# A gated recurrent scan of 512 steps: start-up with a plain float32 input product, a first step without matmuls, and the low parts of the recurrent weights made later

## The chip, the cores and the metric

The kernel runs on one core of a Trainium2 chip. The metric is the device time of one execution in microseconds (us); the time before is the median of three runs. The engines are TensorE (PE in the profile; its weight loads are PEld), VectorE (DVE), ScalarE (ACT), GpSimd (POOL) and SyncE (SP), which issues most of the DMAs. Matmul results land in PSUM, in eight banks of 512 float32 columns; everything else lives in SBUF, with 128 partitions.

## The reference

Two layers act on `x` of 4 x 512 x 256. The first is a gated recurrence over the 512 positions, followed by a feed-forward layer; the second is a mixture of dense experts and a routed layer with 64 experts. Only the recurrence matters here:

```
xz, xr, xh = seq @ W_z, seq @ W_r, seq @ W          # for all positions
vz, vr, vh = video @ C_z + b_z, video @ C_r + b_r, video @ C + b
def step(h, xs):
    z = sigmoid(xzt + h @ U_z + vz)
    r = sigmoid(xrt + h @ U_r + vr)
    hh = tanh(xht + r * h @ U + vh)
    h_new = (1 - z) * h + z * hh
h0 = zeros                                          # 4 x 256
```

`seq` is x (batch 4, 512 steps, width 256) and the state h has 4 x 256 values. Each step needs the state of the step before.

## The kernel before

**Layout.** Features lie on partitions, so the state is 128 partitions x 8 columns (two halves of the width, four of the batch). The steps are cut into spans of 40, the last one of 32. For each span the three input products (gates r, z and candidate, two halves of the output each, so `GROUPS` = 6 products of 160 columns) are made one span ahead and put, scaled and with their biases, into PSUM banks 0 to 5 (`pre`: one pair of banks for each gate, even and odd spans taking turns). The recurrent products are then added to them there.

**Precision.** Float32 inputs are split in two: W and x into a high part in the reduced format float32r (made by ACT, `W_part[0]`, `x_part[0]`) and the remainder (made by DVE, `W_part[1]`, `x_part[1]`, by `low_weights` and `low_inputs`). A product is then three matmuls (`MEET`): high x high, low x high, high x low. `input_product` yields 6 x 2 x 3 = 36 of them for a span. The recurrent weights U are scaled by a power of two and split into float16: `Us[:, g, 0]` by ACT (L419), `Us[:, g, 1]` by DVE (L609). A recurrent product (`recur`) is 12 matmuls of 4 columns: 8 for the high part of the state with both parts of U, 4 for its low part.

**Start-up** (nothing recurrent runs yet). TensorE: clears banks with a product of ones and zeros (`clear(0)`, L804), condition product (L838, 12 matmuls of 4 columns), biases (L843), then the input product of span 0 (L889 to L896) into banks 6 and 7. Two small products are worked in between: after 12 of the 36 matmuls the turning of the peaks of |U| (L892), after 24 the product with ones that spreads the scales to all partitions (L895). Then come `clear(1)`, a wait for all three low parts of U (`s_ulo`) and one for all six seeded products (`s_first`). DVE: low parts of inputs and weights (L544, L549), peaks of U (L557), bias sums (L561, L563), the chain that makes scales out of peaks (L567 to L582), their reading from PSUM (L586 to L589), `vb` (L593), then alternately a scaled copy of an input product into `pre` (`first_span`, L600) and a low part of U (L609), three pairs, then three more copies, then `low_inputs` of span 1. ACT: high parts of inputs and weights (L409, L415), high parts of U (L419).

**A step** (the loops from L489, L749 and L905). TensorE adds to the r gate's columns the step's own part (L908, L910) and then the state's product for z (L913, L915); ACT takes tanh for r (L493) and twice for z (L495, L496) and scales z (L498); DVE makes (1 + r) h, high and low (L755, L617), and the kept part (1 - z) h (L762, L764, L768); TensorE multiplies the reset state with U for the candidate (L929, L931), ACT takes its tanh (L500), DVE makes z times candidate, high and low (L772, L773, L617) and the new state in its several forms (L781 to L792). TensorE also adds the kept part's product for the next r (L945, L947), one matmul of the next span's input product in each step (`ahead`), and in later spans the feed-forward layer's matmuls of the span before. Semaphores `s_rp`, `s_zp`, `s_cp` tell ACT that r, z and candidate are ready in PSUM. Every engine works its queue in the order of the source; that order is written out by hand.

## Time and profile before

| | us |
|---|---|
| median of 3 runs | 2144.11 (2141.66 to 2145.39) |
| the profiled execution | 2145.97 |
| its span, first to last instruction | 2144.2 |
| TensorE busy in the span | 2104.4 (98%) |
| DVE busy | 1577.6 (74%) |
| ACT busy | 1014.0 (47%) |
| first recurrent tanh (ACT, L493) | starts at 22.09 |
| spacing of the first steps | 1.99 |

The span runs from the first to the last instruction of the profiled execution. "Busy" means that the engine has an instruction in flight; TensorE's instructions overlap one another, so the share says that work is recorded, not that the array is full. A start time in a row is counted from the start of the span. Where an instruction had to wait, a row has in brackets how long the engine was idle before it and who released it. The clock line of the page gives the granted TensorE clock in 40 equal slices, 9 standing for nine tenths or more of the full 2.4 GHz.

### The profile page before, as it was taken

To read this page: it belongs to the slowest core of one execution; us is meant where nothing else is said; L and a number is where in the kernel's file an instruction comes from. 1 tells how busy PE (TensorE), PEld (TensorE's weight loads), DVE (VectorE), ACT (ScalarE), POOL (GpSimd) and SP (SyncE) were. 2 spreads that over 40 slices of the span, in tenths; PEclk is the share of its full clock that TensorE was granted. 3 is DMA by queue.
4 is the path that set the end of the run, shared out by engine and by line. 5 is a ranking of instruction groups with operands and counts; after the bars stand their busy time and mean duration, and the time that the engine had idled before them with its cause. 6 is when DMAs were issued, how large, how long until landed. Compare 5 with 4: busy or idle time off the path is not lost. (4 is left out here: it accounts for less than half of the span.)

```text
span 2144.2 us, 83054 instructions
## 1 busy us (share of the span) xinstructions
PE 2104.4 (98%) x32793; PEld 1974.3 (92%) x32801; DVE 1577.6 (74%) x8997; ACT 1014.0 (47%) x3950; POOL 432.2 (20%) x593
## 2 busy tenths in 40 slices
PE   8999999999999999999999999999999999999997
PEld 7899999999999999999768888766999999999997
DVE  6887877877887887778745555592777777777775
ACT  3555555555555555555555777532222222222221
POOL 0000000000000000000000000444455555555553
PEclk9999999999999999999999999999999999999999
DMA  3001000000000000000003322313888888888882
GB/s 126 4 4 44 4 4 4 4 4 4 4 4 4 4 4 4 4 4 4 3 1 106 100 79 79 128 48 139 274 274 269 282 269 272 284 264 277 280 263 58
DMA packets 55559, 213.73 MB, mean 100 GB/s; under 512 B 11578, under 2 KB 40960, under 8 KB 46976
## 3 DMA queue, kind: packets, MB, share of 16 engines
q1 hardware_dynamic: 36276, 184.41, 23.5%
q0 software_dynamic: 17408, 23.61, 5.8%
q8 instruction: 257, 4.21, 0.8%
q14 instruction: 134, 1.10, 0.2%
q10 hardware_dynamic: 1484, 0.40, 0.1%
HBM read 192.82 MB, written 15.57 MB: 97 GB/s over the span
## 5 line engine op out<-in xcount | busy, mean ns | idle before, releaser
L1849 PE MATMUL bank<-xe,ring 128*128 128x160 f32 x3072 | 438.6, 299 | 0.7 <-DVE xe L1899 0.7
L1849 PEld LDWEIGHTS bank<-xe,ring 128*128 128x128 f32 x3072 | 422.9, 190 | 0.9 <-issue 0.9
L1892 DVE STREAM_TRANSPOSE turned<-ye 32x64 f32<-32x64 f32 x1240 | 291.4, 235 | 16.2
L854 PEld LDWEIGHTS bank<-keep_part,Us 128*128 128x128 f16 x6132 | 276.5, 111 | 1.8 <-DVE keep_part L768 0.4
L854 PE MATMUL bank<-keep_part,Us 128*128 128x4 f16 x6132 | 260.0, 170 | 0.5 <-DVE keep_part L768 0.3
L1877 ACT ACTIVATE gate_f<-bank 128x160 f32<-128x160 f32 x384 | 116.4, 303 | 285.8 <-PE bank L1849 278.3
L854 PE MATMUL bank<-raw,Us 128*128 128x4 f16 x6144 | 241.9, 167 | 2.0 <-issue 1.1
L1804 POOL DMA_INDIRECT out_rows<-res,to_row x128 | 192.3, 1503 | 234.2 <-DVE res L1911 201.6
L493 ACT ACTIVATE r_h<-bank 128x8 f32<-128x8 f32 x512 | 92.3, 180 | 292.0 <-PE bank L854 292.0
L523 POOL TENSOR_TENSOR hist<-ring,unscale 128x128 f32<-128x128 f32 x32 | 16.4, 513 | 1042.2 <-DVE ring L786 1042.2
L1858 PE MATMUL bank<-mid,ring 128*128 128x160 f32 x1536 | 220.9, 300 | 2.1 <-issue 2.1
L1858 PEld LDWEIGHTS bank<-mid,ring 128*128 128x128 f32 x1536 | 213.5, 191 | 2.3 <-issue 2.3
L823 PE MATMUL bank<-in_part,W_part 128*128 128x160 f32 (+1 forms) x468 | 215.3, 474 | 0.0
L1920 DVE TENSOR_TENSOR mid<-bank,gate_f 128x160 f32<-128x160 f32 x384 | 117.6, 318 | 130.8 <-ACT gate_f L1877 123.3
L854 PEld LDWEIGHTS bank<-raw,Us 128*128 128x128 f16 x6144 | 210.1, 105 | 2.5 <-DVE raw L792 1.3
L854 PE MATMUL bank<-rh_high,Us 128*128 128x4 f16 x4096 | 206.3, 172 | 2.9
L854 PE MATMUL bank<-step_high,Us 128*128 128x4 f16 x4096 | 189.5, 168 | 3.8 <-issue 0.8
L854 PEld LDWEIGHTS bank<-rh_high,Us 128*128 128x128 f16 x4096 | 165.1, 112 | 26.6 <-DVE rh_high L755 14.7
L498 ACT ACTIVATE z_cand<-tz,lift 128x8 f32<-128x8 f32 x512 | 155.5, 304 | 16.5
L854 PEld LDWEIGHTS bank<-step_high,Us 128*128 128x128 f16 x4096 | 148.6, 105 | 9.2 <-DVE step_high L772 2.6
L772 DVE TENSOR_TENSOR step_high<-z_cand 128x8 f16<-128x8 f32 x512 | 89.2, 174 | 80.2 <-ACT z_cand L500 70.7
L1097 PE MATMUL bank<-x_part,weights_part 128*128 128x512 f32 x576 | 136.7, 395 | 2.2 <-DVE x_part L1288 2.2
(275 smaller groups left out, 4042.2 us busy)
## 6 DMA issues: line engine op xcount, KB each, us to landing
ring<-in_ew SPq DMA_DIRECT2D x64, 2304.0 KB
raw<-in_L_cond_ew SPq DMA_DIRECT2D x16, 1024.0 KB, 6.6
ctx_rows<-rows SPq DMA_DIRECT2D x2, 1280.0 KB, 6.7
dense_w<-in_L_ffn_W SPq DMA_DIRECT2D x2, 1024.0 KB, 9.3
dense_w<-in_L_cond_sw SPq DMA_DIRECT2D x2, 1024.0 KB, 6.5
out_rows<-orow SPq DMA_DIRECT2D x4, 512.0 KB, 2.9
out_rows<-res,to_row POOLq DMA_INDIRECT x128
xT<-in_xT SPq DMA_DIRECT2D x2, 864.0 KB, 10.0
```

Of the source, the lines that this page charges most:

```text
L493: nc.scalar.activation(r, pre_of(0, q, jj), ACT.Tanh, scale=inv[0]).then_inc(s_r, 1)
L498: nc.scalar.activation(z, tz[:], ACT.Identity, scale=2.0 ** (STATE_EXP - 1), bias=lift[:, 0:1]).then_inc(s_z, 1)
L772: nc.vector.tensor_tensor(step_high[:, :, 2], z, cand, ALU.mult).then_inc(s_shi, 1)
L823: last = nc.tensor.matmul(product(span, n), W_part[w][:, g, k, m * P:(m + 1) * P], steps_of(x_part[x], span)[:, k], start=(k == 0 and i == ...
L854: last = nc.tensor.matmul(pre[g][q][:, jj, m, :], Us[:, g, p, k, m * P:(m + 1) * P], x[part][:, k * B:(k + 1) * B], start=False, stop=Fals ...
L1097: last = nc.tensor.matmul(up[f % len(up)][:], w[i][:, k, f * P:(f + 1) * P], x[j][:, k], start=(k == 0 and i == 0 and j == 0), stop=(k == ...
L1804: nc.gpsimd.indirect_dma_start(out=out[:, :], out_offset=bass.IndirectOffsetOnAxis(ap=to_idx[c][:, 0:1], axis=0), in_=res[e % 2][c][:], in ...
L1849: last = nc.tensor.matmul(bank[f % UPS][:, s_ * CAP:(s_ + 1) * CAP], w1[u][:, k, s_ * FFN + f * P:s_ * FFN + (f + 1) * P], xe[e % 2][:, k] ...
L1858: last = nc.tensor.matmul(bank[6 + e % 2][:, d * CAP:(d + 1) * CAP], w2[u][:, f, d * P:(d + 1) * P], mid[e % 2][:, f], start=(f == 0), sto ...
L1877: nc.scalar.activation(gate[:, f % 2], bank[f % UPS][:, CAP:2 * CAP], ACT.Silu).then_inc(s_silu, 1)
L1892: last = nc.vector.transpose(y[:, :, q, :], ye[e % 2][q * SQ:(q + 1) * SQ, :, j * SQ:(j + 1) * SQ])
L1920: nc.vector.tensor_tensor(mid[e % 2][:, f], bank[f % UPS][:, 0:CAP], gate[:, f % 2], ALU.mult).then_inc(s_mid, 1)
```

## The change

Three things are changed, all in `gru`. First, the input product of span 0 is made of 12 plain float32 matmuls of `W` and `xT`, with no split; the low parts of those inputs are no longer made, and the two small products of the scale chain stand behind the whole product instead of inside it. Second, the first step (m == 1) issues no recurrent matmuls, as its state is zero: TensorE only increments `s_rp`, `s_zp` and `s_cp`, and its product of the kept part for the second step is left out as well. Third, DVE makes all six scaled copies before the low parts of U; two low parts come after them and the third behind the work of the first step, and TensorE waits for each of them where the second step first uses it. The low part of W for the candidate moves behind the scale chain, that of span 1's inputs ahead of it, and ACT copies the weights before the inputs.

```diff
@@ scalar
-                act.wait_ge(s_xe, 32)
-                high_inputs(0)
                 for g in range(GATES):
                     act.wait_ge(s_w[g], 16)
                     nc.scalar.activation(W_part[0][:, g], W[:, g], ACT.Copy).then_inc(s_whi, 1)
+                act.wait_ge(s_xe, 32)
                 high_inputs(1)
@@ vector
-                dve.wait_ge(s_xhi, 1)
-                low_inputs(0, range(KD))
-                for g in range(GATES):
+                for g in range(GATES - 1):
                     low_weights(g)
...
                 last.then_inc(s_peak, 1)
+                dve.wait_ge(s_xhi, 1)
+                low_inputs(1, range(KD))
...
                 last.then_inc(s_sc, 1)
+                low_weights(GATES - 1)
                 dve.wait_ge(s_pt, 2)
...
                 dve.wait_ge(s_vb, 1)
-                for g in range(GATES):
-                    first_span(g)
+                for n in range(GROUPS):
+                    first_span(n)
+
+                def low_recurrent(g):
                     dve.wait_ge(s_uhi, g + 1)
                     nc.vector.scalar_tensor_tensor(out=Us[:, g, 1], in0=U[:, g], scalar=scale[:, g:g + 1], in1=Us[:, g, 0],
                                                    op0=ALU.mult, op1=ALU.subtract).then_inc(s_ulo, 1)
-                for n in range(GATES, GROUPS):
-                    first_span(n)
-                dve.wait_ge(s_xhi, 2)
-                low_inputs(1, range(KD))
+
+                for g in range(GATES - 1):
+                    low_recurrent(g)
...
                     ffn_vector(span, jj)
+                    if j == 0:
+                        low_recurrent(GATES - 1)
@@ tensor
-                pe.wait_ge(s_xlo, KD)
-                for n, f in enumerate(input_product(0)):
-                    if n == 2 * TERMS:
-                        pe.wait_ge(s_peak, 1)
-                        nc.tensor.transpose(bank[5][0:GATES, 0:P], peak[:], ident[:]).then_inc(s_pt, 1)
-                    if n == 4 * TERMS:
-                        pe.wait_ge(s_sc, 5)
-                        nc.tensor.matmul(bank[3][:, 0:3 * GATES], ones[0:GATES, :], scales[:], start=True, stop=True).then_inc(s_pt, 1)
-                    f()
+                pe.wait_ge(s_xe, 32)
+                for n in range(GROUPS):
+                    g, m = n // KD, n % KD
+                    if m == 0:
+                        pe.wait_ge(s_w[g], 16)
+                    for k in range(KD):
+                        last = nc.tensor.matmul(product(0, n), W[:, g, k, m * P:(m + 1) * P], steps_of(xT, 0)[:, k],
+                                                start=(k == 0), stop=(k == KD - 1))
+                    last.then_inc(s_xw, 1)
+                pe.wait_ge(s_peak, 1)
+                nc.tensor.transpose(bank[5][0:GATES, 0:P], peak[:], ident[:]).then_inc(s_pt, 1)
+                pe.wait_ge(s_sc, 5)
+                nc.tensor.matmul(bank[3][:, 0:3 * GATES], ones[0:GATES, :], scales[:], start=True, stop=True).then_inc(s_pt, 1)
...
                 clear(1)
-                pe.wait_ge(s_ulo, GATES)
                 pe.wait_ge(s_first, GROUPS)
+                for s_ in (s_rp, s_zp, s_cp):
+                    pe.sem_inc(s_, 1)
...
-                        pe.wait_ge(s_shi, m)
-                        recur(0, q, jj, step, 0)
-                        pe.wait_ge(s_slo, m)
-                        recur(0, q, jj, step, 1).then_inc(s_rp, 1)
...
+                        if m == 2:
+                            pe.wait_ge(s_ulo, 1)
+                        if m > 1:
+                            pe.wait_ge(s_shi, m)
+                            recur(0, q, jj, step, 0)
+                            pe.wait_ge(s_slo, m)
+                            recur(0, q, jj, step, 1).then_inc(s_rp, 1)
+                        if m == 2:
+                            pe.wait_ge(s_ulo, 2)
...
-                        if m < S:
+                        if 1 < m < S:
```

The products for z and for the candidate are put under `if m > 1` in the same way, the candidate's with a wait for the third low part at m == 2. The counts in the waits on `s_xhi` and `s_xlo` are one span lower throughout, since span 0 no longer increments them.

## Rows read from the trace of the kernel before

**Rows 1.** The page: TensorE's granted clock in 40 equal slices.
```profile
PEclk9999999999999999999999999999999999999999
```

**Rows 2.** Instructions in order of time, start-up: start, us, engine, line, operation.
```profile
3.80 5.28 PE L838 MATMUL bank<-condT,C 128*128 128x4 f32 x24 [0.58 <-DMA condT<-in_condT]
...
9.53 2.85 PE L823 MATMUL bank<-in_part,W_part 128*128 128x160 f32 x12
...
13.27 0.37 PE L892 MATMUL bank<-ident,peak 128*3 128x128 f32 x1 [0.89 <-DVE peak L557]
...
13.68 0.28 DVE L567 TENSOR_REDUCE peaks<-bank 3x1 f32<-3x128 f32 x1 [0.18 <-PE bank L892]
...
14.65 0.48 DVE L582 TENSOR_SCALAR scales<-ident,peaks 3x3 f32<-3x3 f32 x3
...
16.06 0.59 PE L895 MATMUL bank<-scales,ones 3*128 3x9 f32 x2
...
16.69 0.17 DVE L586 COPY scale<-bank 128x6 f32<-128x6 f32 x1 [1.57 <-PE bank L895]
...
17.09 1.95 ACT L419 ACTIVATE Us<-U,scale 128x512 f16<-128x512 f32 x3 [6.99 <-DVE scale L589]
17.31 0.39 DVE L600 SCALAR_TENSOR_TENSOR bank<-bank,scale,vb 128x160 f32<-128x160 f32 x1
...
18.81 0.74 DVE L609 SCALAR_TENSOR_TENSOR Us<-U,scale,Us 128x512 f16<-128x512 f32 x1
...
19.68 1.06 PE L804 MATMUL bank<-zeros,ones_bf 128*128 128x512 bf16 x2 [0.24 <-issue]
...
20.42 0.97 DVE L600 SCALAR_TENSOR_TENSOR bank<-bank,scale,vb 128x160 f32<-128x160 f32 x3
```

**Rows 3.** The same view, first step and start of the second.
```profile
22.09 0.18 ACT L493 ACTIVATE r_h<-bank 128x8 f32<-128x8 f32 x1 [3.05 <-PE bank L854]
...
22.30 0.17 DVE L755 SCALAR_TENSOR_TENSOR rh_high<-r_h,ring 128x8 f16<-128x8 f32 x1 [0.45 <-ACT r_h L493]
...
23.29 0.17 DVE L772 TENSOR_TENSOR step_high<-z_cand 128x8 f16<-128x8 f32 x1 [0.17 <-ACT z_cand L500]
...
23.87 0.17 DVE L792 SCALAR_TENSOR_TENSOR raw<-ring,raw 128x8 f16<-128x8 f32 x1
...
24.28 0.17 DVE L755 SCALAR_TENSOR_TENSOR rh_high<-r_h,ring 128x8 f16<-128x8 f32 x1 [0.24 <-ACT r_h L493]
```

**Rows 4.** The same view, DVE in a step that holds one 512-element operation.
```profile
29.85 0.17 DVE L792 SCALAR_TENSOR_TENSOR raw<-ring,raw 128x8 f16<-128x8 f32 x1
29.94 0.68 DVE L622 TENSOR_REDUCE peak<-dense_w 128x1 f32<-128x512 f32 x1
30.53 0.16 DVE L755 SCALAR_TENSOR_TENSOR rh_high<-r_h,ring 128x8 f16<-128x8 f32 x1
```

**Rows 5.** Matmuls of 160 columns: order of time, then groups (busy us, mean ns).
```profile
9.84 2.55 PE L823 MATMUL bank<-in_part,W_part 128*128 128x160 f32 x11
...
1495.81 3.14 PE L1858 MATMUL bank<-mid,ring 128*128 128x160 f32 x11
...
1499.73 2.47 PE L1849 MATMUL bank<-xe,ring 128*128 128x160 f32 x17
...
L823 PE MATMUL bank<-in_part,W_part 128*128 128x160 f32 x36 | 8.5, 422 | 0.0
...
L1858 PE MATMUL bank<-mid,ring 128*128 128x160 f32 x12 | 3.3, 469 | 0.0
...
L1849 PE MATMUL bank<-xe,ring 128*128 128x160 f32 x29 | 4.4, 306 | 0.0
```

**Rows 6.** TensorE after the recurrence, in order of time; then a window with its granted clock.
```profile
1073.07 0.84 PE L1077 MATMUL bank<-raw,ffn_parts 128*128 128x128 f16 x12 [0.34 <-DVE raw L1292]
1076.15 2.93 PE L1097 MATMUL bank<-x_part,weights_part 128*128 128x512 f32 x6 [2.24 <-DVE x_part L1288]
...
1075.90:1079.20 3.30, 3.05 (x7) 2.47 (x8) 0.20 (x1) 1.32 (x2) 0.00 (x0) 0.50 0.00 0
```

More of the change, by code:

```diff
@@ L795, in _ @@
                     if span + 2 < SPANS and jj in lows:
-                        dve.wait_ge(s_xhi, span + 3)
+                        dve.wait_ge(s_xhi, span + 2)
                         low_inputs(span + 2, (lows.index(jj),))
                     ffn_vector(span, jj)
+                    if j == 0:
+                        low_recurrent(GATES - 1)
             @block.tensor
@@ L814, in one @@
                                     if k == 0 and i == 0:
-                                        if span == 0 and m == 0:
+                                        if span == 1 and m == 0:
                                             pe.wait_ge(s_wlo, g + 1)
@@ L906, in _ @@
                         m = STARTS[span] + jj + 1
-                        pe.wait_ge(s_shi, m)
-                        recur(0, q, jj, step, 0)
-                        pe.wait_ge(s_slo, m)
-                        recur(0, q, jj, step, 1).then_inc(s_rp, 1)
-                        state = [part_of(p, STARTS[span] + jj - 1) for p in range(2)]
-                        pe.wait_ge(s_hhi, m)
-                        recur(1, q, jj, state, 0)
-                        pe.wait_ge(s_hlo, m)
-                        recur(1, q, jj, state, 1).then_inc(s_zp, 1)
+                        if m == 2:
[7 more added lines that the diff above has]
+                            pe.wait_ge(s_ulo, 2)
+                        if m > 1:
+                            state = [part_of(p, STARTS[span] + jj - 1) for p in range(2)]
+                            pe.wait_ge(s_hhi, m)
+                            recur(1, q, jj, state, 0)
+                            pe.wait_ge(s_hlo, m)
+                            recur(1, q, jj, state, 1).then_inc(s_zp, 1)
                         (up_beside_z, up_later), (down_beside_z, down_later) = up_products(span, jj), down_products(span, jj)
@@ L918, in _ @@
                             if jj == 0:
-                                pe.wait_ge(s_xlo, (span + 2) * KD)
+                                pe.wait_ge(s_xlo, (span + 1) * KD)
                             ahead[jj]()
@@ L927, in _ @@
                                 ffn_down(span, f, d, i)
-                        pe.wait_ge(s_rhhi, m)
-                        recur(2, q, jj, reset, 0)
-                        pe.wait_ge(s_rhlo, m)
-                        recur(2, q, jj, reset, 1).then_inc(s_cp, 1)
+                        if m == 2:
+                            pe.wait_ge(s_ulo, 3)
+                        if m > 1:
+                            pe.wait_ge(s_rhhi, m)
+                            recur(2, q, jj, reset, 0)
+                            pe.wait_ge(s_rhlo, m)
+                            recur(2, q, jj, reset, 1).then_inc(s_cp, 1)
                         if span:
@@ L947, in _ @@
                             recur(0, nq, njj, kept, 1)
-                        else:
+                        if m == S:
                             keep_busy(nc, bank[5], ones_bf, idle_rows[:], 4)
```

## Prediction

> **What bounds the kernel now.** I read the page's busy shares and clock line first, then the order of instructions in the opening 25 us, then single forms. By the busy shares (98% in the table above) TensorE nearly always has work in flight, so no long wait is left to remove. The change touches the 21.5 us of start-up and the first two recurrent steps; the other 510 steps, the dense layer and the experts keep their instructions. So the question is when the second step's candidate work starts after the edit. The point to watch is DVE's L755 of the second step, at 24.28 us [rows 3].
>
> What sets the start-up is read in [rows 2]. The input product (36 matmuls, three groups of 12) starts at 9.53. After its first 12 TensorE waits 0.89 us for DVE's peak search, turns the peaks at 13.27, DVE works on them from 13.68 to 15.13, and the scales go out by the ones product at 16.06, held back by the second group of 12. DVE reads them at 16.69; then come three pairs of a scaled copy (0.39 us) and a low part of U (0.74 us), and three more copies, to 21.39. TensorE's first recurrent matmuls follow, ACT's tanh at 22.09, DVE's first step at 22.30 [rows 3].
>
> The clock line shows 1.00 from the start [rows 1], but TensorE's spacing says otherwise. Two 512-column products of L804 take 1.06 us at 19.68 [rows 2], 0.53 each; six of 512 columns at a granted 0.50 take 2.93 us [rows 6], 0.49 each. So I take start-up to run at 1.2 GHz, the lower level.
>
> **The change part by part.**
> (1) *Input product.* Before: 11 matmuls in a row last 2.55 us and one 0.42, so they are (2.55 - 0.42)/10 = 0.213 us apart [rows 5]. A condition product of only 4 columns takes 5.28/24 = 0.220 us [rows 2], so weight loads pace this, not the 160 columns. After: 12 plain float32 matmuls, which a trace shows as two records each (L838 is 12 in the source, 24 in the trace). This very form, float32 with 160 columns, stands in the experts at a granted 0.50: 11 in 3.14 us, one lasting 0.47, so (3.14 - 0.47)/10 = 0.267 us a record [rows 5]. 24 records cost 6.4 us against 36 x 0.213 = 7.7 us. The start stays at 9.53: inputs and first weights have been used by ACT and DVE before that, and the engine is on the condition and bias products until then. At 1.2 GHz the last record starts at 9.53 + 0.30 (the first spacing, 2.85 - 2.55) + 22 x 0.267 = 15.70.
> The Trainium skill ("FP8 and Floating Point Precision", TensorE Precision Notes) gives true float32 four passes through the array. By that rule alone 12 x 4 = 48 passes would replace 36 and the product would grow by a third. The trace disagrees: the reduced form isn't paced by its columns here.
>
> (2) *The scale chain moves behind the product.* It was interleaved with it; now the peaks wait until the turn at 15.70 + 0.27 = 15.97. From there the steps of [rows 2] repeat: 0.41 to L567 (16.38), 1.50 to the ones product (17.88: DVE's part ended at 15.13, so it could have gone out at 15.18, 1.50 after L567), 0.63 to L586 (18.51), 0.62 to the first scaled copy (19.13). So the first copy is 1.82 us later than before. The low part of W for gate 2 is put into DVE's 0.7 us wait for the ones product; by its size (512 elements, like L622's 0.68 us in [rows 4]) it hides, with under 0.1 us to spare.
>
> (3) *U's low parts leave the chain.* The six copies run back to back, 0.29 us apart ((0.97 - 0.39)/2), last start 19.13 + 5 x 0.29 = 20.58. ACT's high parts start 0.40 after L586 and take 1.95, to 20.86. TensorE's clear, 0.43 us a product, is over by 20.8. Then two low parts, each 0.74 long and let go 0.09 before its end, as L622 in [rows 4] (0.68 long, the next operation 0.59 after its start): 2 x 0.65. DVE is free for step 0 at 20.58 + 0.29 + 1.30 = 22.17. Before it was 22.30.
>
> (4) *First step without matmuls.* Its products with a zero state leave: 24 of L854 ahead of the gates, 12 for the candidate, 12 for the next r. TensorE now only signals; ACT starts near 21.2 instead of 22.09 and has all its results near 21.9, before DVE comes. So DVE no longer waits for the candidate between L755 and L772, 0.99 us in [rows 3]. Unheld I estimate 0.77 (the four operations between start 0.21, 0.13, 0.06 and 0.26 after one another, and 0.11 more). L772 falls at 22.94 instead of 23.29, L792 at 23.52 instead of 23.87.
>
> (5) *The third low part sits behind step 0 on DVE.* Queued behind it is L755 of step 1, and behind that TensorE's candidate matmuls. Unhindered, L755 comes 0.41 us after L792 [rows 3]. With a 512-element operation in between, [rows 4] has 0.09 before it and 0.59 for it; the low part makes that 0.09 + 0.65 = 0.74. L755 of step 1 falls at 23.52 + 0.74 = 24.26, against 24.28.
>
> The sum at 1.2 GHz is -0.02 us. The 1.3 us less of TensorE work and the missing first step buy nothing: the scale chain, now behind the product, and three low parts on DVE take the room. *At nothing:* the low part of the second span's inputs (0.55 us) lies in DVE's wait before 16.38; uncovered it costs its 0.55. Step 1's waits on the low parts are met before they are looked at; a bubble of some 0.3 us in its z part is behind the candidate. ACT's reordered copies have been done since 10.2 in the old order, and nothing asks for them before the second span's product.
>
> (6) *The clock inside the product.* In the experts, at a granted 0.50, this form ran back to back from 1495.81, and from 1499.73 it runs at the upper level (17 in 2.47 us, one 0.30): (2.47 - 0.30)/16 = 0.136 us a record [rows 5]. The new product is 6.4 us of just that work. A record at 2.4 GHz saves 0.131 us. If the level rises as late as there (some 3.4 us in) or later, 11 to 0 records gain, 1.5 to 0 us, all of it on the chain of (2). I take the middle, 0.7 us. The bounds are nothing and 24 x 0.131 = 3.1 us.
>
> Forecast: -0.02 - 0.7, about -0.7 us. The profiled execution took 2145.97 us around a span of 2144.2; by the sum it becomes 2145.3. The median of the runs is 1.86 us below it, so 2143.4. What measurement can tell from no change is about 0.2%, 4.3 us: the forecast is no change.
>
> **The rivals.**
> *A: the clock stays at 1.2 GHz.* 2144.1. For it: the old product and L838's 5.3 us did not raise it. Against: this form did, in the experts. Chance 0.25.
> *B: the upper level, once reached, holds through the recurrent steps.* Each step has two stretches in which four matmuls of 4 columns follow a low part of DVE's on the chain. Halving about 0.027 us each and 0.02 us of latency gives 0.07 us a stretch, 0.15 a step, times 511 some 75 us; latency alone 20. Time 2069 to 2124. Against: the level fell to 0.50 by 1075.9, when 12 matmuls of 128 columns (1536 columns) stood before an idle 2.24 us [rows 6], 500 columns a us over both; a step streams 48 x 4 + 160 = 352 columns in 1.99 us. Chance 0.04. The Trainium skill ("TensorE: Matmul & The Clock Gate", Why this matters for your kernels) has the clock kept up as long as no long idle gaps stand between bursts, and by that rule B would hold; the fall after a gap of 2.24 us speaks against leaning on it.
> *C, slower: the two passes of plain float32 don't overlap with span 0's inputs,* which are read as 4 runs of 40 columns, the experts' as 160 in a row. At its whole 0.47 us a record costs 0.207 more, 24 of them 5.0 us: 2149.1. It decides beyond 0.2% from a spacing of 0.267 + 4.3/24 = 0.446 us. Against: the reduced form reads the same runs and overlaps. Chance 0.03.
> *D: start-up gains all of TensorE's saving.* The old product ends at about 16.65 + 2.85 = 19.5 with its breaks, the new one at 16.1: 3.4 us, 2140.7, if the chain behind it were not tight. Against: the chain as added up, all from rows. Chance 0.08.
>
> **How the numbers follow.** Forecast 0.60 (2142.6 to 2144.1), A 0.25, B 0.04, C 0.03, D 0.08. Faster by over 0.2% (under 2139.8): B and 0.02 for what I don't see, 0.06. Slower (over 2148.4): C and 0.01, 0.04. Within: 0.90. The range takes in the forecast, A and D, and a scatter of the runs of some 2 us above: 2140.8 to 2146.2.
>
> **What would show it.** In the changed trace: product records 0.267 us apart from 9.5, going to 0.136 before the end (if not, A); the peaks' turn at 14.5 to 16.0; DVE's first L755 between 20.7 and 22.2 with no wait for ACT after it; L755 of the second step at 22.8 to 24.3, with DVE busy right up to it; then steps 1.99 us apart, as now. A period under 1.95 would be B, a spacing over 0.44 in the product C, a first copy before 17.5 D. I would be wrong if something after 25 us changes its pace.

## The result and the profile after

The changed kernel takes 2139.76 us (median of 20 runs, 2137.93 to 2142.94). The kernel before was run 20 times beside it, with a median of 2142.86, not the 2144.11 of its first three runs. The ratio is 0.9987, with an interval of 0.9981 to 0.9993: 2.8 us less, between 1.5 and 4.1 (the two medians differ by 3.1). I had forecast 0.7 us less, from a base that was 1.25 us too high; the measured time lies below my range. The profiled execution took 2138.56 us around a span of 2136.7, so this pair of spans differs by 7.5 us, far more than the medians do.

The start-up of the changed kernel, in order of time (start, us, engine, line, operation). The line numbers have moved: L897 is the initial product, L901 the peaks' turn, L611 the low parts of U, L756 the first DVE operation of a step (L755 before), L793 its last (L792 before), L492 ACT's tanh for r.

```profile
9.66 5.40 PE L897 MATMUL bank<-xT,W 128*128 128x160 f32 x24
...
14.89 0.27 PE L901 MATMUL bank<-ident,peak 128*3 128x128 f32 x1
...
15.20 0.28 DVE L566 TENSOR_REDUCE peaks<-bank 3x1 f32<-3x128 f32 x1 [1.15 <-PE bank L901]
...
16.70 0.39 PE L903 MATMUL bank<-scales,ones 3*128 3x9 f32 x2 [1.53 <-DVE scales L581]
...
17.76 1.85 DVE L600 SCALAR_TENSOR_TENSOR bank<-bank,scale,vb 128x160 f32<-128x160 f32 x6
...
17.78 0.82 PE L807 MATMUL bank<-zeros,ones_bf 128*128 128x512 bf16 x3 [0.70 <-DVE vb L593]
...
19.52 1.41 DVE L611 SCALAR_TENSOR_TENSOR Us<-U,scale,Us 128x512 f16<-128x512 f32 x2
19.83 0.18 ACT L492 ACTIVATE r_h<-bank 128x8 f32<-128x8 f32 x1 [0.35 <-PEq L909]
...
20.84 0.17 DVE L756 SCALAR_TENSOR_TENSOR rh_high<-r_h,ring 128x8 f16<-128x8 f32 x1
...
22.30 0.17 DVE L793 SCALAR_TENSOR_TENSOR raw<-ring,raw 128x8 f16<-128x8 f32 x1
22.39 0.74 DVE L611 SCALAR_TENSOR_TENSOR Us<-U,scale,Us 128x512 f16<-128x512 f32 x1
...
23.05 0.17 DVE L756 SCALAR_TENSOR_TENSOR rh_high<-r_h,ring 128x8 f16<-128x8 f32 x1
```

The 24 records of the product take 5.40 us, where [rows 2] had three groups of 12 and two breaks between 9.53 and about 19.5. The peaks are turned at 14.89, L600 starts at 17.76 (17.31 before) and its six copies run on end; the second step's L756 comes at 23.05, against 24.28 in [rows 3]: 1.23 us earlier, with DVE busy right up to it. Two narrower windows on the product show the clock, first up to 13.3 us and then from 13.7. The first row is slow, the second fast:

```profile
9.66 4.04 PE L897 MATMUL bank<-xT,W 128*128 128x160 f32 x14
...
13.53 1.52 PE L897 MATMUL bank<-xT,W 128*128 128x160 f32 x10
```

Taking off one record's own duration (0.47 and 0.30, as in [rows 5]) leaves (4.04 - 0.47)/13 = 0.275 us apart, the longer first spacing included, and (1.52 - 0.30)/9 = 0.136. The trace has its first clock record at 13.51 us, so the clock line now shows the level of the recurrence. The page's line:

```profile
PEclk6555555555555555555599999999999999999999
```

And one window over the recurrence (busy times of PE, PEld, DVE, ACT and POOL with their counts, then granted clock, DMA share, GB/s):

```profile
20.40:1060.00 1039.60, 1029.64 (x26109) 995.94 (x26108) 833.74 (x6499) 599.23 (x3016) 16.48 (x32) 0.50 0.02 6
```

So the level rose inside the product, held to 20.34 us and was 0.50 throughout the recurrence, with TensorE "busy" for 99% of it. The median step period is 1.99 us in both kernels, so I read the 1.00 of [rows 1] in the same stretch of the kernel before as a missing record.

**What lies behind 25 us.** I compared the starts of ACT's first tanh step by step. Two places differ. In the kernel before, the period of the step that starts at 184.58 us is 3.26 us instead of 2.01; in the changed kernel all periods there are 2.01. TensorE in the kernel before, in order of time:

```profile
185.96 0.19 PE L854 MATMUL bank<-raw,Us 128*128 128x4 f16 x2 [1.14 <-issue]
```

And ACT's tanh around that place:

```profile
184.58 0.18 ACT L493 ACTIVATE r_h<-bank 128x8 f32<-128x8 f32 x1 [0.29 <-PE bank L854]
187.84 0.18 ACT L493 ACTIVATE r_h<-bank 128x8 f32<-128x8 f32 x1 [0.81 <-PE bank L854]
```

TensorE stood still for 1.14 us in mid-product and waited for nothing that the profile shows. Against that, the changed kernel has more small pauses of DVE, 0.13 to 0.37 us each and put down to issue as well, at other steps than before; DVE in the changed kernel:

```profile
116.92 0.17 DVE L793 SCALAR_TENSOR_TENSOR raw<-ring,raw 128x8 f16<-128x8 f32 x1 [0.30 <-issue]
```

The excess of the steps that are over 0.12 us longer than the fastest execution of the same step adds up to 3.9 us in the changed kernel and, without the stall, to 2.4 in the kernel before. The last tanh of the recurrence comes at 1057.00 against 1058.58, 1.6 us earlier. The other 5.9 us of the two spans' difference lie in the dense stage (294.3 us before, 291.6 after, from TensorE's first instruction to the next stage's) and the experts (660.3 and 657.0), whose code is the same.

**Why those two stages differ.** In the kernel before the granted clock falls to 0.50 for 3.41 us in the dense stage ([rows 6] shows the stretch) and again in the experts; in the changed kernel it does neither. In the experts the fall follows an idle 2.08 us of TensorE. The kernel before at 14 products, with the row of a window on them as above, and the changed kernel at the same 14:

```profile
1495.24 3.72 PE L1858 MATMUL bank<-mid,ring 128*128 128x160 f32 x14 [2.08 <-issue]
...
1495.80:1499.00 3.20, 3.20 (x13) 3.20 (x13) 0.00 (x0) 0.01 (x1) 1.70 (x4) 0.50 0.89 361
```

```profile
1489.48 2.17 PE L1875 MATMUL bank<-mid,ring 128*128 128x160 f32 x14 [0.55 <-DVE mid L1937]
```

The 17 profiles below bear this out. The dense stage takes 291.4 to 292.0 us in the eight where the clock does not fall in it, 294.0 to 294.6 in the six with a fall of 3.41 us and 294.8 to 295.4 in the three with one of 6.83. The experts take 660.3 us in the three profiles (before, best, loads_later) that have an idle of 2.0 to 2.1 us and then the fall, 658.4 in after_dve_pad with that idle alone, and 656.0 to 657.6 in the other 13. What brings the idle time of the experts is open: ACT's operation ahead of it comes late, and its wait, 2.55 to 2.60 us in these four profiles, is put down to no engine of the core.

### The profile page after: what moved, and what is told of

It reads as the page before. It is cut to its first block and busy times, and to the rows that moved or that the text cites. A ratio compares the mean times of both kernels' runs of the same rounds, so it can differ in the third digit from the quotient of the medians.

```text
span 2136.7 us, 82947 instructions
## 1 busy us (share of the span) xinstructions
PE 2096.3 (98%) x32741; PEld 1965.9 (92%) x32741; DVE 1576.0 (74%) x8995; ACT 1013.7 (47%) x3949; POOL 432.2 (20%) x593
## 3 DMA queue, kind: packets, MB, share of 16 engines
q0 software_dynamic: 17408, 23.61, 5.9%
## 5 line engine op out<-in xcount | busy, mean ns | idle before, releaser
L1909 DVE STREAM_TRANSPOSE turned<-ye 32x64 f32<-32x64 f32 x1240 | 291.4, 235 | 16.2
L492 ACT ACTIVATE r_h<-bank 128x8 f32<-128x8 f32 x512 | 92.7, 181 | 290.1 <-PE bank L857 289.7
L826 PE MATMUL bank<-in_part,W_part 128*128 128x160 f32 (+1 forms) x432 | 206.7, 478 | 1.6 <-DVE bank L600 1.6
```

The lines of the kernel that those rows point to most:

```text
L492: nc.scalar.activation(r, pre_of(0, q, jj), ACT.Tanh, scale=inv[0]).then_inc(s_r, 1)
L826: last = nc.tensor.matmul(product(span, n), W_part[w][:, g, k, m * P:(m + 1) * P], steps_of(x_part[x], span)[:, k], start=(k == 0 and i == ...
L1909: last = nc.vector.transpose(y[:, :, q, :], ye[e % 2][q * SQ:(q + 1) * SQ, :, j * SQ:(j + 1) * SQ])
```

## The experiments

The table gives, from the profiled execution of each kernel, the turn of the peaks, DVE's first operation of the second step ("step 2"), the stall of TensorE near 185 us (its longest idle time put down to issue in the recurrence), the sum of the small pauses as defined above, ACT's last tanh, the lengths of dense stage and experts, and the ratio to the kernel before on the same chip with its interval. All in us.

| kernel | turn | step 2 | stall | pauses | last tanh | dense | experts | ratio |
|---|---|---|---|---|---|---|---|---|
| before | 13.27 | 24.28 | 1.1 | 2.4 | 1058.58 | 294.3 | 660.3 | |
| same_before | 13.31 | 24.32 | 1.8 | 2.4 | 1059.17 | 295.0 | 656.9 | 1.0007 (0.9998 to 1.0016) |
| again_before | 13.44 | 24.44 | 1.0 | 2.4 | 1058.98 | 294.0 | 656.0 | 0.9998 (0.9989 to 1.0007) |
| after | 14.89 | 23.05 | none | 3.9 | 1057.00 | 291.6 | 657.0 | 0.9987 (0.9981 to 0.9993) |
| same_after | 14.71 | 22.87 | none | 3.9 | 1057.11 | 294.6 | 657.6 | 0.9981 (0.9972 to 0.9990) |
| again_after | 14.94 | 23.09 | none | 3.9 | 1056.89 | 291.7 | 656.2 | 0.9985 (0.9976 to 0.9994) |
| product_only | 14.86 | 24.70 | 1.1 | 3.9 | 1060.01 | 291.6 | 656.9 | 1.0011 (1.0002 to 1.0020) |
| step_only | 14.25 | 24.51 | none | 2.3 | 1057.27 | 294.0 | 657.2 | 0.9997 (0.9988 to 1.0006) |
| without_product | 13.65 | 24.32 | none | 2.4 | 1057.08 | 291.4 | 656.9 | one time, 2138.21 |
| product_and_step | 15.85 | 24.94 | 0.9 | 3.9 | 1060.25 | 292.0 | 656.0 | 1.0007 (0.9998 to 1.0016) |
| turn_inside | 13.43 | 21.97 | none | 3.8 | 1055.48 | 294.0 | 656.8 | 0.9989 (0.9980 to 0.9998) |
| twice_product | 17.86 | 26.02 | none | 3.9 | 1059.16 | 291.9 | 656.8 | one time, 2140.74 |
| after_padded | 14.33 | 22.48 | 1.2 | 3.9 | 1057.47 | 295.4 | 657.0 | 1.0000 (0.9991 to 1.0009) |
| before_padded | 14.21 | 25.22 | none | 2.4 | 1059.62 | 291.8 | 657.1 | 0.9998 (0.9988 to 1.0007) |
| after_dve_pad | 15.39 | 23.61 | none | 2.4 | 1056.98 | 294.8 | 658.4 | 0.9991 (0.9982 to 1.0000) |
| best | 13.30 | 21.83 | none | 2.4 | 1054.95 | 294.1 | 660.3 | 0.9980 (0.9971 to 0.9989) |
| loads_later | 14.20 | 25.21 | 0.9, at 236 | 2.4 | 1058.90 | 291.8 | 660.3 | 1.0000 (0.9991 to 1.0009) |

**Scatter: same_before.** The kernel before without an edit.

> The kernel before, unchanged, as a measure of scatter. Start-up theory (the change acts only up to the second step, the rest of the difference between the two profiled spans, 7.5 us, is scatter of later stages): L755 of the second step at 24.28 us again, while the dense stage (294.0 us in the trace of before, 291.4 in after) and the experts (660.3 and 657.1) come out differently from before by 1 to 3 us although nothing was changed. Rival (the change makes the later stages faster): dense 294 and experts 660 again, within 0.5 us. Time within 0.1% of before for both.

Dense came out at 295.0 and the experts at 656.9, over 3 us under the first trace. The code was the same, so that much of the 7.5 us says nothing of the change: the clock did not fall in these experts. The stall near 185 us was there again, 1.8 us long.

**The parts alone: product_only.** The product and the order around it as changed; the rest as before, DVE's alternating copies and low parts among it.

```diff
+                for n in range(GROUPS):
+                    for k in range(KD):
+                        last = nc.tensor.matmul(product(0, n), W[:, g, k, m * P:(m + 1) * P], steps_of(xT, 0)[:, k], ...
...
                 pe.wait_ge(s_ulo, GATES)
```

> Part 1 alone: the input product of span 0 in plain float32 with the scale chain behind it; the first step keeps its matmuls and the low parts of U stay between the copies. Clock theory (the level rises inside the product, near 13.5 us): turn of the peaks at 14.9, first scaled copy at 17.8 instead of 17.31, so L755 of the second step at 24.7 instead of 24.28, 0.4 us later. If the product did not raise the clock here: turn at 16.0, L755 at 26.1. Rival (the product is where the gain comes from): L755 before 23.8. Time within 0.1% of before in the first and last case.

24.70, as added up; the clock rose at 13.3 us here too. By itself the faster product makes the start later, since the scale chain went behind it. The stall stayed (1.1 us). The time is 0.1% over before, and the recurrence ends at 1060.01, later than in the three profiles of the kernel before.

**step_only.** `if m > 1` around the first step's products and the three signals, nothing else.

> Part 2 alone: the first step issues no recurrent matmuls (their operand is zero), everything ahead of it as before. Start-up theory: copies end at 21.39 as before, ACT's first tanh at 21.6 instead of 22.09, candidate ready by 22.4, L755 of the second step at 23.55, 0.7 us earlier than before. Rival (DVE, not TensorE or ACT, sets the first step even here): L755 at 24.2 or later. The clock stays at the lower level until the recurrence is over.

24.51 looks like a miss of 1 us, but the peaks were turned 0.98 us later than before (14.25), as DVE's peak search had started later. From the turn to step 2 it is 10.26 us against 11.01: 0.75 us gained, as expected. Two things I had not expected: the stall near 185 us is gone, and the pauses stay at before's 2.4 or so. With that the recurrence ends at 1057.27, nearly as early as in the changed kernel (1057.00), from this part alone. It is one profile, and the times (0.9997) do not show it.

**without_product** (parts 2 and 3) and **product_and_step** (parts 1 and 2).

```diff
 without_product
-                pe.wait_ge(s_xe, 32)
-                for n in range(GROUPS):
+                pe.wait_ge(s_xlo, KD)
+                for n, f in enumerate(input_product(0)):
 product_and_step
-                for n in range(GROUPS):
-                    first_span(n)
+                for g in range(GATES):
+                    first_span(g)
+                    ...
```

> Parts 2 and 3 without part 1: no matmuls in the first step and the low parts of U moved, but the input product of span 0 stays split in 36 matmuls with the scale chain inside it. Added up from rows: the last three copies wait for the third group of matmuls, at 19.45, and end at 20.3; two low parts to 21.65; L755 of the second step at 23.9, 0.4 us earlier than before (24.28) and 0.8 later than the changed kernel (23.05). The clock stays low. Rival (moving the low parts is worth nothing): 24.3 or later.

Step 2 is at 24.32, which by itself is where the rival had it, but the turn was 0.38 late (13.65). From the turn it is 10.67 us, against 11.01 before: 0.34 gained, against the 0.4 expected. With step_only's 10.26 beside it, moving the low parts cost 0.4 us here: DVE stood idle for 1.19 us before the last three copies, waiting for the slow product, and the low parts came only after them. The recurrence ends at 1057.08 even so, as in the changed kernel, since the pauses stayed at 2.4.

> Parts 1 and 2 without part 3: plain product, no matmuls in the first step, but the three low parts of U stay between the first copies, all ahead of the first step. From rows: first copy at 17.76 as in the changed kernel, last copy 3.70 later and done at 21.85, tanh of the first step near 22.0, L755 of the second step at 24.0, so moving the low parts is worth 0.9 us of the 1.2. Rival (the low parts cost the same wherever DVE does them): 23.2 or earlier. TensorE's count is that of the changed kernel, so no stall near 185 us; DVE pauses of 3.9 us.

The turn was late once more (15.85: the identity and the biases had landed late, and the product started at 10.96). From there to step 2 it took 9.09 us, against 8.16 in the changed kernel: moving the low parts is worth 0.93, as expected. My statement that no stall would be there was wrong: TensorE idled 0.90 us at 184.96. So the count of instructions is not all; when they are reached against the loads matters too.

**The clock's share: twice_product.** Each pair of matmuls is issued twice, the second overwriting the first.

```diff
+                    for again in range(2):
                         for k in range(KD):
```

> The changed kernel with each pair of matmuls of the initial input product issued twice, the second pair overwriting the first: 48 records instead of 24. Clock theory: the level rises some 14 records in, and the rest runs 0.136 us apart; the turn of the peaks comes 24 x 0.136 = 3.3 us later, at 18.2, and L755 of the second step at 26.3. Rival (records are 0.267 or 0.213 apart at either level, and the earlier end of the product has another cause): turn at 20.0 or later.

The turn came 2.97 us later (17.86) for 24 more records; the level had risen 0.6 us sooner than in the changed kernel, at 12.88. That makes 2.97 = 24 x 0.136 less about 0.3 for the earlier rise. Records of this form cost 0.136 us once the level is up, and the rival's 20.0 is excluded.

**The stall: after_padded, before_padded.** 60 matmuls of four columns, zeros by ones into a cleared bank, are added where TensorE idles; 80 in the other kernel, in three idle places.

```diff
+                for _ in range(60):
+                    nc.tensor.matmul(bank[5][:, 0:4], ones_bf[:], zeros[:, 0:4], start=False, stop=False, skip_group_check=True)
```

> The changed kernel with 60 added matmuls of 4 columns (zeros added to zeros) right behind TensorE's signals of the first step, where it is idle from 19.65 to 21.9 us: they put back the 120 TensorE records that the change took out ahead of the second step. Instruction theory (before, TensorE stood still for 1.1 to 1.8 us near 185 us, put down to issue, because its next block of instructions arrives late behind the bulk loads of 174 to 186 us; in the changed kernel the blocks fall differently by count): L755 of the second step at 23.05 as in the changed kernel, but the period of the step that begins near 184 us grows from 2.0 to 3.2 us or more, and the time is about 1.2 us over the changed kernel. Rival (the stall went because the steps come 1.2 us earlier against the bulk loads, or by chance): all periods there at 2.0, time as the changed kernel.

TensorE in after_padded, in order of time:

```profile
184.94 0.30 PE L857 MATMUL bank<-raw,Us 128*128 128x4 f16 x6 [1.16 <-issue]
```

And ACT there:

```profile
183.66 0.18 ACT L492 ACTIVATE r_h<-bank 128x8 f32<-128x8 f32 x1 [0.29 <-PE bank L857]
186.86 0.18 ACT L492 ACTIVATE r_h<-bank 128x8 f32<-128x8 f32 x1 [0.81 <-PE bank L857]
```

The stall is back, period 3.20. The start of step 2 (22.48) shows that the recurrence began even earlier than in the changed kernel. The time went from 0.9987 to 1.0000 of before, more than the stall's 1.2 us. The rest stays open; the two ratios come from different sets of runs, and in the profiled execution the clock fell for 6.83 us in the dense stage (295.4).

> The kernel before with 80 added matmuls of 4 columns on zeros, in TensorE's idle times of the start-up (40 while it waits for the first inputs, 16 ahead of the peaks' turn, 24 behind the clear of the odd banks). Nothing is taken out. Instruction theory: 160 records more shift the blocks of instructions as the 96 fewer of the run with part 2 alone did (they differ by one block of 256), so the stall near 185 us is gone (period 2.0 there instead of 3.26) while L755 of the second step stays at 24.3: some 1.2 us faster than before, ratio about 0.9994. Rival (by chance or by the earlier start): stall of 1.1 us or more there as before, ratio 1.000.

The period of that place is back to 2.01; ACT in before_padded:

```profile
185.61 0.18 ACT L493 ACTIVATE r_h<-bank 128x8 f32<-128x8 f32 x1 [0.29 <-PE bank L856]
187.62 0.18 ACT L493 ACTIVATE r_h<-bank 128x8 f32<-128x8 f32 x1 [0.81 <-PE bank L856]
```

Adding work that computes nothing removed the stall. In the time it doesn't show (0.9998): the profiled execution had a late turn (14.21), and the interval of 0.1% each way can't tell 1.2 us from nothing. Nor does it show in the recurrence as a whole: from step 2 to the last tanh it is 1034.40 us here and 1034.30, 1034.85 and 1034.54 in the three profiles of the kernel before. At step 80 this execution was 1.15 us ahead of the first of them; then it lost about 3 ns in each step. Why is open.

**What it waits behind: loads_later.**

```diff
                 sp.wait_ge(s_w16lo, 2 * PAIRS * LOWS)
+                sp.wait_ge(s_h, 101)
                 load_next(sp)
```

> The kernel before, with SyncE holding back the bulk loads of the shared layer's weights until step 100 is done (they ran from 174 to 186 us). Theory (the stall near 185 us is TensorE's instruction block arriving late behind these loads): period of that step back to 2.0 us; the loads then run near 230 to 242 us and a stall of up to 1.8 us may stand there instead, if a block is due in them at the wrong moment. Rival (the stall belongs to that point of the program, whatever is being loaded): the period near 185 us stays at 3.2 us or more.

Windows of the same columns. The kernel before, over the loads and over their densest part:

```profile
174.00:186.00 12.00, 10.71 (x281) 10.34 (x278) 8.17 (x65) 5.74 (x30) 0.00 (x0) 1.00 0.62 180
...
177.00:183.40 6.40, 6.25 (x167) 6.01 (x165) 4.52 (x37) 3.34 (x18) 0.00 (x0) 1.00 0.94 306
```

The changed kernel, with the same loads and no idle time of TensorE:

```profile
174.00:186.00 12.00, 12.00 (x313) 11.56 (x311) 8.81 (x73) 6.48 (x34) 0.00 (x0) 0.50 0.60 180
```

loads_later, at the old place (3 GB/s) and at the new one (165 GB/s):

```profile
174.00:186.00 12.00, 11.85 (x306) 11.45 (x304) 8.79 (x72) 6.40 (x35) 0.00 (x0) 1.00 0.01 3
...
229.00:242.00 13.00, 12.13 (x312) 11.97 (x309) 9.98 (x80) 7.20 (x36) 0.00 (x0) 1.00 0.52 165
```

And TensorE at the new place, in order of time:

```profile
236.47 0.47 PE L824 MATMUL bank<-in_part,W_part 128*128 128x160 f32 x1 [0.87 <-issue]
```

The stall left 185 us with the loads and stands at 236 now, in the midst of them. So it needs two things: bulk loads that keep the DMA engines 94% busy, and TensorE reaching the end of what it has of its instructions meanwhile. The 16 KB transfers of the instruction queue fit this: in the kernel before they come every 5.1 us (median), but 7.9 apart (175.4 to 183.3) across the loads; in the changed kernel one came at 177.2, and the next at 183.4. All 17 profiles agree: across the loads that spacing is 7.2 to 8.4 us in the seven with a stall and at most 6.8 in the ten without, and in each of the seven TensorE starts again 1.3 to 1.5 us after the late transfer has ended. The Trainium skill ("Runtime: NRT & Kernel Launch", Instruction fetch mechanics) has each engine's instructions refilled in blocks of 256 by a DMA queue of its own, and calls the cost mostly hidden. The trace agrees with the block size: 257 transfers of 16 KB for TensorE's 65594 recorded instructions, 255 each. Hidden it was not, for 0.9 to 1.8 us.

**DVE's pauses: after_dve_pad.**

```diff
+                for c in range(2):
+                    nc.vector.memset(unread[:, c:c + 1], 0.0)
```

> The changed kernel with two added one-column memsets on DVE at 1.4 us, where DVE waits for inputs; they put back the two DVE instructions that part 1 took out. Instruction theory (which steps meet a pause of 0.13 to 0.37 us depends on how many DVE instructions come before them: sums of 2.4 us in all kernels with the old count, 3.7 to 3.9 us in all with two fewer): L755 of the second step at 23.05, pauses at steps 76, 114, 190, 205 as in the kernel before and not at 31, 46, 61, 167, 175, the recurrence 1.5 us shorter, last tanh at 1055.6 instead of 1057.0. Rival (part 1 causes the pauses in another way, by the later input parts): pauses as in the changed kernel, last tanh 1057.0.

The pauses stand at before's steps (76, 114, 190, 205, ...) and add up to 2.4. From step 2 to the last tanh it is 1033.37 us against 1033.95 in after, 1034.24 in same_after and 1033.80 in again_after, so of the expected 1.5 only 0.4 to 0.9 is in the total. Where the rest went is open. The last tanh (1056.98) missed my number for a second reason: the clock rose only at 14.53 in this execution, so the turn was at 15.39.

**A better start: turn_inside, best.**

```diff
+                    if n == GATES:
+                        pe.wait_ge(s_peak, 1)
+                        nc.tensor.transpose(bank[5][0:GATES, 0:P], peak[:], ident[:]).then_inc(s_pt, 1)
```

> The changed kernel with the turning of the peaks moved from behind the product to its middle, after three of six output groups; the other small product stays at the end. Chain theory (after the product the scale chain, turn to first copy 2.87 us, is what DVE waits for): turn at 13.4 instead of 14.89, first copy near 16.3 instead of 17.76, L755 of the second step near 21.6 instead of 23.05; time 1.5 us under the changed kernel, ratio to before about 0.998. Rival (the clock: the break in the product keeps the level low, so the product ends at 16.2 and the copies wait for it): first copy at 17.8 or later, no gain on the changed kernel.

Turn 13.43, step 2 at 21.97: the chain theory holds, at 1.08 us instead of the 1.5. DVE was still at other work when the turn came, so its first operation on the peaks started 0.63 us after the turn, against 0.31 in the changed kernel, and the ones product went out at 15.64, 0.1 us later behind DVE's scales than there. The clock rose in spite of the break. The recurrence ends 1.5 us earlier than in the changed kernel, but the time (0.9989) does not show it.

> The changed kernel with the peaks' turn in the middle of the product and the two DVE memsets: both gains together. L755 of the second step at 21.97 as in turn_inside, no stall near 185 us, pauses of 2.4 us, last tanh of the recurrence at 1054.0, 4.6 us earlier than in the kernel before and 3.0 earlier than in the changed one; ratio to before about 0.998. Rival (the gains at the start are lost again before the recurrence ends): last tanh later than 1056.

The last tanh is at 1054.95, 3.6 us earlier than before and 1.9 to 2.2 earlier than in the three profiled executions of the changed kernel; I had expected 1054.0. The median is 2140.50 against 2141.75 of the changed kernel on the same chip, and the intervals of the two ratios overlap: a better start by the traces, not shown to be faster by the times.

**The changed kernel again: same_after, again_after, again_before.**

> The changed kernel, unchanged, beside the other three on one chip. Theory as it stands (start-up 1.2 us, the stall near 185 us 1.2 to 1.8, against it some 1.5 us more of small pauses of DVE during the recurrence, the dense stage and the experts pure scatter): last tanh of the recurrence within 0.5 us of 1057.0, dense stage either near 291.5 or 294 to 295 us, ratio to before 0.9985 to 0.9995. Rival (the change makes the later stages faster as well): dense near 291.5 and experts 657.0 again.

> The changed kernel, once more. Scatter theory: last tanh at 1057.0 to 1057.3, dense stage and experts within the same ranges as again_before, ratio to before between 0.9985 and 0.9995, centred on 1.8 us less. Rival (the change is worth more than its effect up to the end of the recurrence): ratio under 0.9983 again.

> The kernel before, once more, as the partner of again_after. Scatter theory: stall of more than 1 us near 185 us, pauses of 2.4 us, last tanh at 1058.5 to 1059.5, dense stage anywhere from 291.4 to 295.4 us, experts from 656.8 to 660.3.

The last tanh came at 1057.00, 1057.11 and 1056.89 against 1058.58, 1059.17 and 1058.98. The means differ by 1.91 us. The ratios are 0.9987, 0.9981 and 0.9985, 2.8, 4.1 and 3.2 us. Two of the intervals take in 1.9 us (0.9991), the one of same_after just not. Of the 1.91 us, 1.34 lie ahead of step 2 (24.35 against 23.00 in the mean) and 0.57 in the recurrence.

## Why the prediction was wrong

*Start-up at 1.2 GHz, step by step.* It held closely where the level did not matter: six copies with 1.46 us from the first start to the last (1.45 forecast), 1.62 from the last copy's start to DVE's step 0 (1.59), 1.46 for step 0 (1.35), 0.75 for the low part behind it (0.74). All four places that I had named in the start-up fell inside their windows (turn 14.89, first step 20.84 with no wait for ACT, second step 23.05, then steps of 1.99). The start-up came out at -1.23 instead of -0.7.

*The clock term was mis-sized.* I took the middle of 0 to 1.5 us. The level rose 14 records in, at 13.51 us in after and between 12.48 and 14.53 in all kernels with the plain product, so 10 records gained 0.131 each: the term measured 1.3 us and not 0.7. With the product's start 0.13 late, the turn came at 14.89 instead of 15.97. The two small products behind it were cheaper as well (L903 to the first copy 1.06 us, 1.25 forecast). That the row in the experts would carry over was right.

*The step that failed: "the other 510 steps keep their instructions", so nothing after 25 us changes its pace.* They keep them, but 120 records on TensorE and 2 instructions on DVE are gone ahead of them, so they stand elsewhere in the blocks in which they are fetched (pads of the same count put the stall back in after_padded and the pauses back to their old steps in after_dve_pad). That took out a stall of 1.0 to 1.8 us near 185 us and put the DVE pauses at other steps, 1.5 us more in sum. From step 2 to the last tanh the three profiles of the changed kernel are 0.57 us shorter in the mean (1033.80 to 1034.24 against 1034.30 to 1034.85). The two sums would nearly cancel, so they are not the costs. Sorting all 17 profiles by the two gives for the same stretch 1032.8 to 1033.4 us with neither the stall nor the longer pauses (1034.4 in before_padded), 1033.2 to 1034.2 with the pauses, 1033.7 to 1034.9 with the stall, and 1035.0 to 1035.3 with both. By the means of these groups I estimate 1.1 to 1.5 us for a stall and 0.5 to 0.9 for the longer pauses. So of the 2.1 us between the forecast -0.7 and the measured -2.8, about 0.6 lie in the start-up (by the means, -1.34), 0.6 in the recurrence, which I had at nothing, and the rest beyond the last tanh. My list of what could move held only what the change computes, not where its instructions lie.

*The base.* The median of the first three runs was 1.25 us over that of 20. Against the right base my forecast would have been 2142.2, and with the whole 1.9 us up to the last tanh 2141.0. The range suffered from it too: its lower edge, 2140.8, was rival D's time, with nothing below it for the scatter of the runs, of which I allowed for some above. Moved down by 1.25 us it would have reached to 2139.55 and held the measured 2139.76.

*The rivals.* A fell (the level rose), B fell too: it was back to 0.50 at 20.3 us, after TensorE had stood idle for 1.53, 0.70 and, from 18.6 to 20.2, 1.61 us with little work in between, and stayed there. The Trainium skill's advice on idle gaps ("TensorE: Matmul & The Clock Gate", Why this matters for your kernels) is not enough by itself: here the level fell without a single gap longer than 1.61 us, in [rows 6] with none longer than 2.24. C fell: the strided inputs overlap at 0.267 and 0.136. D was nearest in size (-3.4) but not in kind: start-up gained 1.23.

*What lies beyond the last tanh.* The traces give 1.9 us up to there, the times 2.8 to 4.1. Falls of the granted clock account for most of the difference in the one set of runs where I can sort them. Each execution lists its mean granted clock. Among the seven profiles with the split product it is 0.998 in the two without a fall in the dense stage or the experts, 0.997 in the three with 3.41 us of it and 0.996 in the two with 6.83 in all. The executions of the kernel before that ran beside again_after sort the same way: medians of 2140.29 us at 0.998 (9 runs), 2142.40 at 0.997 (6) and 2143.44 at 0.996 (11). The changed kernel lists 0.754 in its two profiles without a fall; the six of its 11 executions there that list 0.754 have a median of 2138.02. Without falls, then, it is 2.3 us less (an estimate from 9 and 6 executions), near the 1.9 of the traces. The rest of the 3.2 there is how often the clock fell.

*What stays open.* Whether the change has a hand in that. The falls in the dense stage come 10 us after the level has risen, as at 1075.9 in [rows 6], and the 2.24 us of idle time ahead of that place stand in all 17 profiles, the eight without a fall included. The kernel before had a fall there in three of three profiles, the changed one in one of three. An earlier end of the recurrence might make it rarer, but turn_inside and best, with earlier ends still, had it, and the share of executions at 0.998 went from 0 of 11 (same_before) to 5 of 11 (again_before) without any edit. I don't count it to the change. Open too is which part the 1.9 us need: step_only and without_product end the recurrence at 1057.27 and 1057.08, one profile each, without the plain product.

## What to carry to other kernels

Work out the start-up of a chained kernel as a list of starts, each from the one before by a spacing read in the trace, and give the level of the clock a line of its own in it: a dense float32 product was here both the work and what raised the clock. When instructions are added or removed anywhere in a long unrolled program, look for idle time put down to issue at unrelated places, above all under bulk loads; pads of no use in idle time move it, and so does moving the loads. And compare stages, not spans, and read the granted clock of each: two executions of the same kernel differed by over 3 us in the experts alone, by a fall of the clock and the idle time before it, which the 40 digits of the clock line do not show.

## What the runs showed of the hardware

- TensorE stood still for 0.9 to 1.8 us when a bulk load of weights (306 GB/s over 6.4 us) put the 16 KB transfers of its instructions 7.2 to 8.4 us apart instead of 5; at up to 6.8 us it did not. The same kernel with the loads moved stalled at the new place.
- TensorE counted as busy for 99% of the recurrence (1029.64 of 1039.60 us) and was granted 0.50 all the while; its products of four columns never raised the clock, 24 records of 160 columns in float32 raised it in each of the 10 profiles of kernels that have them.
- The clock line shows 1.00 until the first change is recorded, also where the level is 0.50; the spacing of a known product tells which (0.275 and 0.136 us on the two sides of the first record at 13.51).
- A fall of the granted clock to 0.50 for 3.41 us made the dense stage 2 to 3 us longer; with the same idle 2.24 us ahead of that place it came in 9 of 17 profiles.
- The arrival of the first inputs scatters by about 1 us between executions (turn of the peaks at 13.3 to 14.3 with the split product), as much as the whole gain of the start-up.
